# A perceiver block on one core: the next batch's queries get a buffer of their own and are split in mid-batch, the context is split two tiles ahead, the maximum is spread before the sum, and the denominators and weight pieces move

## What is computed

```python
q = rmsnorm((layernorm(x) @ Wq).reshape(B, Sq, H, D), gq)
k = rmsnorm((ctx @ Wk).reshape(B, Skv, H, D), gk)
v = (ctx @ Wv).reshape(B, Skv, H, D)
attn = softmax(einsum('bqhd,bkhd->bhqk', q, k) / sqrt(D))
x = x + einsum('bhqk,bkhd->bqhd', attn, v).reshape(B, Sq, H * D) @ Wo
x = x + causal_attention(layernorm(x)); x = x + ternary_ffn(layernorm(x))
```

## Time and profile before

| | |
|---|---|
| median of 3 runs (range) | 1662.11 us (1657.1 to 1662.15) |
| the profiled execution's own time, its span | 1663.32 us, 1661.5 us |
| mean granted TensorE clock | 0.962 |
| TensorE busy | 1508.6 us, 91% |
| VectorE, ScalarE, GpSimd busy | 1232.7, 994.7, 169.6 us |
| chain that ended last, by engine | PE 64%, DVE 15%, issue 12%, ACT 6% |

### The profile page before, as it was taken

How to read it: one execution, slowest core, us unless ns; L and a number is a source line. 1 busy time by engine, 2 the same in 40 slices (tenths; PEclk the granted TensorE clock), 3 DMA queues, 4 the chain that set the end, 5 groups by cost and what they waited for, 6 DMA issues and landing times.

```text
span 1661.5 us, 21718 instructions
## 1 busy us (share of the span) xinstructions
PE 1508.6 (91%) x6830; PEld 1212.2 (73%) x6872; DVE 1232.7 (74%) x1949; ACT 994.7 (60%) x3683; POOL 169.6 (10%) x121
## 2 busy tenths in 40 slices
PE   7978888999999999899989997999799866997898
PEld 5756666887888788678868886788588655885687
DVE  7636676878878888887878877777878896667543
ACT  4555665666767677666666775676576564632432
POOL 2200000002000200200020002000200202012333
PEclk9989999999999999999989998999999988998999
DMA  5431112111111211021112111111111051650000
GB/s 169 157 133 42 57 42 79 38 42 60 57 38 36 86 38 40 25 92 38 38 56 65 35 38 54 60 38 36 54 38 27 18 189 38 222 203 2 1 1 26
DMA packets 85074, 104.14 MB, mean 63 GB/s; under 512 B 7128, under 2 KB 67040, under 8 KB 83168
## 3 DMA queue, kind: packets, MB, share of 16 engines
q1 hardware_dynamic: 77664, 95.41, 18.2%
q10 hardware_dynamic: 7296, 7.34, 1.3%
HBM read 80.71 MB, written 22.02 MB: 62 GB/s over the span
## 4 chain that ended last, share of the span: by engine, by line
PE 64%; DVE 15%; issue 12%; ACT 6%; DMA 2%; POOL 1%; ACTq 0%; POOLq 0%; SPq 0%; DVEq 0%; another core or an unknown queue 0%
PE ps L35 20%; PE ps L36 19%; PE ps L37 19%; ACT ps L1323 3%; PE ps L694 2%; PE ps L695 2%; DVE run_max L903 2%; DVE fq_lo L41 1%; DVE p_lo L41 1%; PE ps L712 1%; PE ps L713 1%; DVE w_q L965 1%; ACT w_scale L1402 1%; DVE ring L885 1%; DVE k_sum L859 1%
## 5 line engine op out<-in xcount | busy, mean ns | idle before, releaser
L35 PE MATMUL ps<-wk_hi,cT_hi 128*128 128x512 f32 x832 | 335.4, 403 | 64.2 <-DVE cT_lo L41 42.6
L1323 ACT ACTIVATE ps<-ps 123x128 f32<-123x128 f32 (+1 forms) x1248 | 324.6, 260 | 108.6 <-PE ps L37 108.5
L36 PE MATMUL ps<-wk_lo,cT_hi 128*128 128x512 f32 x832 | 331.1, 398 | 0.0
L37 PE MATMUL ps<-wk_hi,cT_lo 128*128 128x512 f32 x832 | 328.8, 395 | 0.0
L35 PEld LDWEIGHTS ps<-wk_hi,cT_hi 128*128 128x128 f32 x832 | 159.6, 192 | 103.0 <-DVE cT_lo L41 46.9
L1323 ACT ACTIVATION_READ_ACCUMULATOR ps<-ps 123x1 f32 (+1 forms) x1248 | 230.3, 185 | 0.0
L35 PE MATMUL ps<-p_hi,cn_hi 123*128 123x512 f32 (+1 forms) x416 | 174.4, 419 | 27.3 <-DVE cn_lo L41 23.6
L37 PEld LDWEIGHTS ps<-wk_hi,cT_lo 128*128 128x128 f32 x832 | 159.6, 192 | 35.7
L36 PEld LDWEIGHTS ps<-wk_lo,cT_hi 128*128 128x128 f32 x832 | 160.5, 193 | 32.8
L885 DVE TENSOR_TENSOR ring<-ps,k_rstd 123x1024 f32<-123x1024 f32 (+1 forms) x104 | 127.1, 1222 | 73.6 <-PE ps L37 73.5
L1329 ACT ACTIVATE k_log<-k_mean 123x16 f32<-123x16 f32 (+1 forms) x104 | 22.5, 216 | 250.1 <-DVE k_mean L862 250.1
(11 more groups left out here) (198 smaller groups left out, 2656.6 us busy)
## 6 DMA issues: line engine op xcount, KB each, us to landing
cT_raw<-in_ctxT SPq DMA_DIRECT2D x96, 128.0 KB, 2.2
cn_raw<-in_ctx SPq DMA_DIRECT2D x88, 123.0 KB
w_raw<-in_wguT SPq DMA_DIRECT2D x32, 256.0 KB, 2.7
qk_scratch<-folded ACTq DMA_DIRECT2D x8, 896.0 KB, 4.1
fq_raw<-qk_scratch SPq DMA_DIRECT2D x7, 1024.0 KB, 5.1
ternary_scratch<-w_out SPq DMA_DIRECT2D x48, 128.0 KB, 1.7
pc_scratch<-pc_out SPq DMA_DIRECT2D x6, 1024.0 KB, 5.7
w_bf<-ternary_scratch SPq DMA_DIRECT2D x1, 6144.0 KB, 23.0
```

The lines of the kernel that those rows point to most:

```text
L35: pe.matmul(dst, l_hi, r_hi, start=first, stop=False)
L36: pe.matmul(dst, l_hi, r_lo, start=False, stop=False)
L37: return pe.matmul(dst, l_lo, r_hi, start=False, stop=last)
L1323: done = act.activation(head, head, ACT.Square, accum_out=k_sum[0:n, i, g * GH + h:g * GH + h + 1])
```

## The change

- `fq_hi` and `fq_lo` have two buffers, by batch. Batch b+1's queries are split in batch b, the first half in the step of its tile 4, the second in that of tile 7; `fq_raw` holds one half (batch 0's second half is kept in `run_max`, not used yet then).
- `cT_hi` and `cT_lo` have four buffers and are split two tiles ahead; in a batch's first step after `key_mean`.
- GpSimd spreads the maximum first, then the sum.
- ScalarE takes the sum's logarithm and reciprocal in the batch's second step; VectorE's `sum_refine` moves to the third step, with `evacuate` directly behind it, both behind `numerator_lo` and `low_cn`. The first tile's `exponential` stands behind the context's split.
- Pieces stand in steps 2 to 13, and from batch 1 on at tiles 3, 5, 8, 10 and 12 of each batch, with one more at tile 6 of the last; their raw tile has one buffer. To make room the ring has 14 slots instead of 15.

```diff
-        fq_raw = keys.take("fq_raw", [P, KC, HQ])
+        fq_raw = keys.take("fq_raw", [P, HQ])
...
-        RING = 15
+        RING = 14
...
+        fq_hi = work.take("fq_hi", [P, 2, KC, HQ], F32R)
+        fq_lo = work.take("fq_lo", [P, 2, KC, HQ], F32R)
+        w_raw = work.take("w_raw", [P, BANK])
...
-        piece_slots = list(range(2, LAG_AV))
-        later = NP - len(piece_slots)
-        piece_slots += [LAG_AV + (2 * i + 1) * (N - LAG_AV) // (2 * later) for i in range(later)]
+        FQ_STEPS = (4, 7)
+        piece_slots = list(range(2, TT + 1))
+        piece_slots += [b * TT + t for b in range(1, B) for t in (3, 5, 8, 10, 12)]
+        piece_slots = sorted(piece_slots + [(B - 1) * TT + 6])
...
             low_cT(0)
+            low_cT(1)
...
-                if av and v > 0 and tiles[v][1] == 0:
-                    evacuate(tiles[v][0] - 1)
                 if av:
                     numerator_lo(v)
                     low_cn(v)
                 if num and tiles[u][1] == 0:
                     subtract_max(u)
+                if v > 0 and tiles[v][1] == 0:
+                    sum_refine(tiles[v][0] - 1)
+                    evacuate(tiles[v][0] - 1)
...
-                if s > 1 and s < N and tiles[s][1] == 0:
-                    low_fq(tiles[s][0])
-                if s + 1 < N:
-                    low_cT(s + 1)
+                if s + 2 < N and tiles[s][1] > 0:
+                    low_cT(s + 2)
+                if s < N and tiles[s][0] + 1 < B and tiles[s][1] in FQ_STEPS:
+                    low_fq(tiles[s][0] + 1, FQ_STEPS.index(tiles[s][1]))
                 if s in piece_at:
                     ternary_round(piece_at[s])
-                if av and tiles[v][1] == TT - 1:
-                    sum_refine(tiles[v][0])
                 if s < N:
                     key_mean(s)
+                if s + 2 < N and tiles[s][1] == 0:
+                    low_cT(s + 2)
...
-                if num:
+                if num and tiles[u][1] > 0:
                     exponential(u)
                 if key:
                     key_square(s, 1)
-                if s + 1 < N:
-                    high_cT(s + 1)
-                if s > 1 and s < N and tiles[s][1] == 0:
-                    high_fq(tiles[s][0])
+                if s + 2 < N:
+                    high_cT(s + 2)
+                if num and tiles[u][1] == 0:
+                    exponential(u)
                 if s in piece_at:
                     ternary_abs(piece_at[s])
-                if v >= 0 and tiles[v][1] == TT - 1:
-                    sum_guess(tiles[v][0])
+                if ends:
+                    sum_log(tiles[v][0])
+                if key and tiles[s][0] + 1 < B and tiles[s][1] in FQ_STEPS:
+                    high_fq(tiles[s][0] + 1, FQ_STEPS.index(tiles[s][1]))
...
-                if num and tiles[u][1] == TT - 1:
-                    sum_log(tiles[u][0])
+                if ends:
+                    sum_guess(tiles[v][0])
```

More of the change, by code:

```diff
@@ L100, in perceiver_block @@
         cT_raw = keys.take("cT_raw", [P, 3, KC, P])
-        cT_hi = keys.take("cT_hi", [P, 3, KC, P], F32R)
-        cT_lo = keys.take("cT_lo", [P, 3, KC, P], F32R)
+        cT_hi = keys.take("cT_hi", [P, 4, KC, P], F32R)
+        cT_lo = keys.take("cT_lo", [P, 4, KC, P], F32R)
         sq = keys.take("sq", [P, BANK])
@@ L455, in scores @@
                 b, t, n = tiles[s]
[L456 removed]
+                i, hh = s % 4, slice(half * BANK, (half + 1) * BANK)
                 if half == 0:
@@ L849, in low_cn, with low_fq @@
                 low_part(dve, cn_lo[0:n, s % 2], cn_raw[0:n, s % 3], cn_hi[0:n, s % 2]).then_inc(cn_lo_done, 1)
[L851 to L854, removed]
+            def low_fq(b, k):
+                raw = run_max if b == 0 and k == 1 else fq_raw
+                dve.wait_ge(fq_hi_done, KC * b + k + 1)
+                low_part(dve, fq_lo[:, b % 2, k], raw[:], fq_hi[:, b % 2, k]).then_inc(fq_lo_done, 1)
             def key_mean(s):
@@ L992, in dve_program @@
                         fold_copy(NG - 1, c)
-                    low_fq(0)
+                    for k in range(KC):
+                        low_fq(0, k)
                 if num and tiles[u][1] > 0:
                     subtract_max(u)
-                if av and v > 0 and tiles[v][1] == 0:
-                    evacuate(tiles[v][0] - 1)
                 if av:
@@ L1300, in high_cn, with high_fq @@
                 act.copy(cn_hi[0:n, s % 2], cn_raw[0:n, s % 3]).then_inc(cn_hi_done, 1)
-            def high_fq(b):
+            def high_fq(b, k):
+                raw = run_max if b == 0 and k == 1 else fq_raw
                 if b == 0:
@@ L1305, in high_fq @@
                 else:
[L1306 to L1309, removed]
+                    act.wait_ge(fq_in, 16 * (KC * (b - 1) + k + 1))
+                if b >= 2:
+                    act.wait_ge(scores_mm, TT * (b - 1))
+                act.copy(fq_hi[:, b % 2, k], raw[:]).then_inc(fq_hi_done, 1)
             def key_square(s, g):
@@ L1378, in act_program @@
                 key, num = s < N, 0 <= u < N
+                ends = v >= 0 and tiles[v][1] == TT - 1
                 if key:
                     key_square(s, 0)
-                if num:
+                if num and tiles[u][1] > 0:
                     exponential(u)
@@ L1560, in pool_program @@
             pool.wait_ge(fold_kept, KC * NG)
+            pool.wait_ge(fq_lo_done, KC)
+            pool.memset(run_max[P // 2:], -3.0e38).then_inc(consts, 1)
+            pool.wait_ge(consts, 8)
+            for c in range(KC):
+                pool.wait_ge(fold_out[c], 16 * NG)
             pool.memset(run_sum[P // 2:], 0.0).then_inc(consts, 1)
@@ L1564, in pool_program @@
                 u = s - LAG_P
+                if 0 <= s - 1 < N and tiles[s - 1][1] == TT - 1:
+                    b = tiles[s - 1][0]
+                    pool.wait_ge(maxed, (TT - 1) * (b + 1))
+                    if b > 0:
+                        pool.wait_ge(shifted, b * TT)
+                    pool.partition_all_reduce(col_max[:], run_max[:], P,
+                                              bass.bass_isa.ReduceOp.max).then_inc(max_spread, 1)
                 if 0 <= u < N and tiles[u][1] == TT - 1:
```

70 lines of the change are left out of this document (32 added, 38 removed).

## The result

The changed kernel takes **1616.18 us** (median of four executions, 1613.22 to 1618.78), the kernel before 1662.13 beside it: a ratio of 0.9729, 95% interval 0.9703 to 0.9755. The forecast was 1621, from 1600 to 1645. The profiled execution took 1615.52 us, 47.8 less than that of before. TensorE is busy for 93% of the span where it was 91%.

What follows compares the result with a forecast made beforehand. Matmuls set the pace except at six batch boundaries losing 9.9 us each. Boundaries -37.2, batch 1 -8.9 and +0.2, queries +1.9, loop start -1.2, tail +4.0 sum to -41.2 from 1663.3; median 1621, range 1600 to 1645.

Steps and rivals of the forecast that it cites:

- The boundary: At each of six batch boundaries the loss falls from 9.9 to 3.7 us, -37.2 in all.
- Held `cn_lo`: At a boundary the sum's spread holds `cn_lo` to 18.7 us; the context product wants it at 17.8: 1.0 us.
- Division: In a batch's third step the first half is divided by 31.8 us, wanted at 30.0: 1.8 us of waiting.
- The term for the clock: Waits at a boundary sometimes slow TensorE's clock: 1.7 us, counted at four boundaries in ten, 0.7.
- The whole-instruction hold: Rival, chance 0.05: GpSimd keeps VectorE out for all 6.12 us of the sum's spread; boundary loss 5.4, time 1631.
- What is held: Beside a GpSimd spread, VectorE instructions with two inputs in SBUF are held; no size of its own.
- From the start: A hold begins within 0.66 us of a spread's start and was taken from the start.
- the rival in which it slips through: Chance 0.15: holds begin only 0.6 us into a spread, `cn_lo` escapes, a boundary loses 0 to 1: 1599 to 1605.
- Queries in mid-batch: Splits in steps 4 and 7 are hidden, 0; in batch 0 they are not: +1.9 us, between 0 and 3.
- Start of batch 1: Steps 13 to 15 take 31.1 us instead of 40.0: -8.9, between -5 and -10.
- Start of the loop: Step 1 no longer waits for `cT_lo`, but its third bank waits for ScalarE: -1.2 us, between 0 and -4.
- The tail: After step 104 the maximum's spread and the piece at tile 12 delay VectorE's chain: +4.0 us, between 0 and +6.

Runs made afterwards that it cites:

- the second experiment: The changed kernel with the denominators at their old places, the maximum's spread still first: 1647.26 us.
- the third one: The changed kernel with the sum's spread first again and the denominators at their old places: 1614.62 us.
- the fifth experiment: The changed kernel with each batch's queries split in that batch's own first step, both halves in a row: 1632.56 us.
- the first experiment: The changed kernel with GpSimd's two spreads in their old order, the sum's first: 1609.46 us.

## Why the prediction was right

- **The boundary: right.** Forecast 3.7 us lost, measured 2.5. Held `cn_lo`: predicted 1.0, measured 0.64. Squares in the third step: predicted 0.2, measured none. Division: predicted 1.8, measured 1.85. The term for the clock, 0.7, was zero: waits of 0.33 and 1.57 us left it at 1.00 at all six boundaries, and those of batch 6 before are no rule for it. The term was also worked out wrong: a mean of 0.72 over 12 us is 6.7 us at half the clock and costs up to 3.4, not 3.4 us at half and 1.7; counted so it would have been 1.4. That it came to nothing is part of why the time lies below the 1621. The difference, 1.2 us six times, is the 7.2 us by which steps 26 to 103 came out lower (879.4, the lower edge of the 879 to 900 given). The 9.9 of before is a mean: the three steps took 39.0 us in batch 2 and 49.1 in batch 6, and the wait for `cT_lo` was 3.3 us in batches 2 and 3 and 6.5 only from batch 4 on.
- **The denominators a step later: right, and needed**, since the maximum was put first (1647 without); with the sum first they are worth 1 us.
- **The whole-instruction hold: fell.** `cn_lo` ended at 837.65, 1.3 us before the sum's spread did (832.72 + 6.23). The Trainium skill, SBUF — State Buffer, section "Who interferes with whom", has the loser wait for the whole instruction; here the measurement decides: the sum's spread lets go after some 4.5 of 6.2 us. The profile's spans on GpSimd are rough, but this end is a real one: in the second experiment ScalarE's logarithm, which waits for the sum, starts 0.03 us behind it (854.64).
- **What is held: not complete.** I wrote of two inputs in SBUF. `k_mean`, with one, took 0.87 instead of 0.17 us here, 1.77 and 4.17 in the experiments, and the third one's forecast for the boundary missed by it. The same section of the Trainium skill says that a `tensor_scalar` can contend too and that a `tensor_reduce` never does on this chip; the trace agrees with both (`k_sum` kept its 0.69 beside the maximum's spread).
- **From the start: right at the boundaries.** `cn_lo` started 0.18 us after the sum's spread did and was held in full, so the rival in which it slips through (1599 to 1605) fell. In the tail one did slip through (the last section has it), in a case that no forecast rested on.
- **Queries in mid-batch: the mechanism right, the size off.** Hidden from batch 1 on. In batch 0 steps 4, 5 and 7 took 11.04, 11.17 and 11.04 instead of 10.21, 10.09 and 10.09: +3.0 for the +1.9, at the edge of its bounds. The two steps that split give 1.8 of it; most of the rest is step 5, behind the first split, while step 8, behind the second, took its 10.09. Why they differ is open.
- **Start of batch 1: right**, 30.25 for 31.1 us. **Start of the loop**: -2.4 within its bounds of 0 and -4; step 1 begins 5.3 us earlier, and 3.0 of that are lost again in step 1, where the profile has a wait for ScalarE's squares, as foreseen.
- **The tail: right up to the last batch's first product**, 29.4 us where 28.7 to 30.2 were worked out (+3.9 for +4.0). The other 1.6 us lie in the layers behind it, which took between 322.0 and 326.7 us over the eleven profiled executions of this study; it is no effect of the change that a run here shows.
- **What I gave the change credit for.** The prediction put the whole 6.53 down to lead and queries together. Undone one at a time, the queries at the start cost 2.8 a boundary, a lead of one tile 1.3, the old pieces 3.6, the old denominators about 5; and the order of the spreads, which looked like the heart of it, loses time, 0.6 a boundary. Neither a lead of one tile nor the queries at the start bring back the wait of 6.5 us for `cT_lo` in the second step, so what ended it is not tied to one of them. The costs overlap and do not add up to what the boundary won.

## What to carry to other kernels

In this kernel a long GpSimd instruction holds VectorE's next contending instruction and everything queued behind it. Its price is set by what stands in that queue, so put it beside work that nobody waits for soon. An earlier start by itself is not enough: 1.85 us earlier, it caught `p_lo` instead of `cn_lo` and won 0.6. Place filler work (here the weight pieces) by the same rule: its length is the small part of its price. In a batch's first or second step one went with 4 to 6 us more, in mid-batch it costs 0.23 where the steps beside it have none, and 1.3 between two others. And two edits can be worth more together than their sum: from 1616.2, each alone gives 1609.5 and 1609.6, both give 1596.4.

## What the runs showed of the hardware

- A spread itself gets longer when a contending VectorE instruction is already running as it starts: the maximum's takes 3.23 us where none is, 3.81 beside `fq_lo`, and 4.13 beside `p_lo` in the tail or `fq_lo` in the fifth experiment.
- The hold of VectorE by the maximum's spread ends 1.75 us after the spread's start (`k_mean` ended at 831.51, 1.92 after 829.59, of which it needs 0.17; 1.83 in the first experiment); with `fq_lo` in its way at the start it was 2.35.
- A hold ends before the spread does in every case seen: after 1.75 of 3.23 and about 4.5 of 6.23 us.
- A VectorE instruction can also slip through. The last sum's spread starts 0.18 us behind a `p_lo`; it takes 7.35 us, and the `cn_lo` that starts 0.96 us into it takes its usual 0.41. Beside the maximum's spread in the same position (1269.69) `cn_lo` took 2.12.

```profile
1333.90 1.22 DVE L41 TENSOR_TENSOR p_lo<-ring,p_hi 123x1024 fp32r<-123x1024 f32 x1
1334.08 7.35 POOL L1594 PARTITION_ALL_REDUCE col_sum<-run_sum  x1 [54.17 <-DVE run_sum L933]
...
1335.04 0.41 DVE L41 TENSOR_TENSOR cn_lo<-cn_raw,cn_hi 123x256 fp32r<-123x256 f32 x1
```
